# Single maxima behind each unit of scores and each weighing in the first softmax, in place of twos and threes behind a pair of key blocks

## The reference, cut to what matters

```
h = _layernorm(x) * (1 + ca) + sa
Q, K, V = proj(h)                       # 16 heads of 8, rotary on Q and K
scores = einsum('bhqd,bhkd->bhqk', Q, K) / sqrt(8)
scores = where(causal, scores, -1e10)
att = softmax(scores)                   # x is 4 batches of 512 tokens of 128
x = x + ga * (att @ V @ Wo + bo)
h = _layernorm(x) * (1 + cb) + sb
x = x + gb * ffn(h)                     # 16 experts, top 2
```

## Time and profile before

| | us |
|---|---|
| median of 3 runs | 442.27 |
| lowest, highest | 441.61, 442.72 |
| profiled execution, its own time | 441.48 |
| span of the profiled execution, first to last instruction | 439.70 |
| PE busy in the span | 353.3 |
| DVE busy | 298.0 |
| ACT busy | 242.2 |

### The profile page before, as it was taken

How to read it: one execution, slowest core, us unless ns; L and a number is a source line. 1 busy time by engine, 2 the same in 40 slices (tenths; PEclk the granted TensorE clock), 3 DMA queues, 4 the chain that set the end, 5 groups by cost and what they waited for, 6 DMA issues and landing times.

```text
span 439.7 us, 7235 instructions
## 1 busy us (share of the span) xinstructions
PE 353.3 (80%) x2652; PEld 164.3 (37%) x2684; DVE 298.0 (68%) x596; ACT 242.2 (55%) x291; POOL 111.2 (25%) x151
## 2 busy tenths in 40 slices
PE   0555386888867978999879969998879798879995
PEld 0532142445534444443444434433545323123122
DVE  7479994575878797777576877786549456943342
ACT  1102023344224786887534868875457887858970
POOL 8334720000524020443250204433130023122000
PEclk9996666999989999999998999999999999989999
DMA  8102410000220182554001715551105155704550
GB/s 291 25 1 68 79 46 24 3 5 0 50 29 2 39 106 71 137 143 110 2 25 31 95 51 141 135 133 22 28 0 73 36 144 160 117 2 121 151 135 24
DMA packets 26847, 31.43 MB, mean 71 GB/s; under 512 B 6454, under 2 KB 17718, under 8 KB 26678
## 3 DMA queue, kind: packets, MB, share of 16 engines
q1 hardware_dynamic: 23740, 28.84, 28.3%
q0 software_dynamic: 3072, 2.13, 2.8%
HBM read 3.47 MB, written 1.05 MB: 10 GB/s over the span
## 4 chain that ended last, share of the span: by engine, by line
PE 53%; DVE 19%; ACT 10%; issue 7%; SPq 4%; DMA 4%; POOL 1%; ACTq 0%; DVEq 0%; POOLq 0%
PE acc L1125 17%; PE big L1125 17%; PE misc L1125 17%; ACT ring L657 7%; DVE mx L897 6%; DVE xn L838 3%; DMA q_dense<-nm 2%; PE misc L1144 2%; SPq L425 2%; SPq L446 1%; ACT qk_turned L665 1%; SPq L380 1%; DVE stats L813 1%; DMA q_dense<-qk 1%; ACT L690 1%
## 5 line engine op out<-in xcount | busy, mean ns | idle before, releaser
L657 ACT ACTIVATE ring<-big 128x1024 f32<-128x1024 f32 (+1 forms) x224 | 197.3, 932 | 124.5 <-PE big L1125 123.2
L897 DVE TENSOR_REDUCE mx<-misc 128x1 f32<-128x320 f32 (+7 forms) x154 | 86.9, 589 | 36.0 <-PE misc L1125 34.6
L1125 PE MATMUL acc<-ring,cb 128*32 128x512 f32 x512 | 68.8, 612 | 5.4 <-ACT ring L657 4.4
L1125 PE MATMUL big<-tstack,w1s 128*128 128x512 bf16 x177 | 52.4, 381 | 10.0 <-ACT ring L657 7.1
L1125 PE MATMUL big<-q_dense,k_block 128*128 128x448 bf16 (+7 forms) x249 | 53.4, 320 | 5.2 <-DMA q_dense<-nm 3.1
L1125 PE MATMUL misc<-k_dense,q_block 128*128 128x384 bf16 (+7 forms) x171 | 43.6, 318 | 6.4 <-DVE mx L897 5.9
L1020 DVE SCALAR_TENSOR_TENSOR gm<-acc,cb,gm 128x512 f32<-128x512 f32 x40 | 29.9, 747 | 27.3 <-DMA gm<-wT 14.5
L1125 PEld LDWEIGHTS big<-q_dense,k_block 128*128 128x128 bf16 x256 | 30.8, 148 | 31.1 <-ACT ring L657 14.3
L1125 PEld LDWEIGHTS misc<-k_dense,q_block 128*128 128x128 bf16 x174 | 21.3, 149 | 52.1 <-DVE mx L897 37.0
L1125 PE MATMUL acc<-ring,vals 128*32 128x64 f32 (+7 forms) x512 | 40.1, 421 | 0.4
L1125 PE MATMUL big<-earlier_query,identb 128*128 128x64 bf16 (+2 forms) x176 | 37.0, 210 | 2.5 <-DMA q_dense<-nm 1.8
(11 more groups left out here) (160 smaller groups left out, 486.2 us busy)
## 6 DMA issues: line engine op xcount, KB each, us to landing
gm<-wT SPq DMA_DIRECT2D x64, 256.0 KB
tstack<-tp SPq DMA_DIRECT2D x18, 128.0 KB, 5.1
k_block<-qk_turned POOLq DMA_DIRECT2D x48, 32.0 KB, 3.6
q_dense<-qk SPq DMA_DIRECT2D x24, 64.0 KB
ca<-in_pack_a SPq DMA_DIRECT2D x1, 1155.0 KB, 5.4
k_dense<-qk SPq DMA_DIRECT2D x18, 64.0 KB
xs<-in_x SPq DMA_DIRECT2D x4, 256.0 KB, 8.0
q_block<-qk_turned SPq DMA_DIRECT2D x24, 32.0 KB
```

The lines of the kernel that those rows point to most:

```text
L657: act.activation(dst, src, func, scale=scale).then_inc(s["ring_read"], 1)
L897: dve.tensor_reduce(mx[:, g, k:k + n, blk], src, AX.X, ALU.max).then_inc(s["misc_read"], 1)
L1125: return pe.matmul(dst, lhsT, rhs, start=start, stop=stop)
```

## The change

`WOVEN` is now a table from a slot to units, where a slot is a unit of scores or one weighing. Behind most slots stands one unit of maxima, behind the weighings of key blocks 0 and 1 of each group two. Six units of the first batch move from the softmax into `ALONE` (of 384, 384 and four of 320 columns), one more unit of the second batch moves from `LEFT` into the softmax. `softmax` calls `between` behind each unit of scores and each weighing. PE's wait for batch 1's `k_dense` and `q_block` moves from key block (0, 4) to between `early_scores` and the rest of the softmax.

```
-ALONE = UNITS0[0] + UNITS0[1][:3] + [("mT", 0)] + UNITS0[1][3:10]
-REST = UNITS0[1][10:] + [("mT", 1)]
-WOVEN = {("first", 0, 0): REST[0:3], ("first", 0, 1): REST[3:6], ("first", 0, 2): REST[6:9], ("first", 0, 3): REST[9:12],
...
-LEFT = MAXIMA[30:]
+ALONE = UNITS0[0] + UNITS0[1][:3] + [("mT", 0)] + UNITS0[1][3:16]
+REST = UNITS0[1][16:] + [("mT", 1)]
+SLOTS = [("scores", 0, 4), ("scores", 0, 5), ("weigh", 0, 0), ("weigh", 0, 1), ("scores", 0, 6), ("scores", 0, 7),
...
+TWICE = [("weigh", 0, 0), ("weigh", 0, 1), ("weigh", 1, 0), ("weigh", 1, 1)]
+FIRST_SLOTS = SLOTS[:5]
...
+for slot in SLOTS[5:]:
+    n = 2 if slot in TWICE else 1
+    WOVEN["second", slot] = MAXIMA[at:at + n]
+    at += n
+LEFT = MAXIMA[at:]
...
                                 scores(phase, g * NU + u)
+                                if ("scores", g, u) in between:
+                                    between["scores", g, u]()
                         if len(late) == 2:
-                            weigh(m, phase, *late.pop(0))
-                            weigh(m, phase, *late.pop(0))
+                            for was in late:
+                                weigh(m, phase, *was)
+                                if ("weigh", *was) in between:
+                                    between["weigh", *was]()
+                            late = []
...
-                    if (g, blk) == (0, 4):
-                        for stack in ("k_dense", "q_block0", "q_block1"):
-                            wait_stacked(pe, stack, 2)
...
+            for stack in ("k_dense", "q_block0", "q_block1"):
+                wait_stacked(pe, stack, 2)
+            softmax(0, softmax_at(0), {slot: woven(slot) for slot in SLOTS})
```

## The result

| | before | changed |
|---|---|---|
| median of 7 runs each, us | 442.27 | 438.89 |
| lowest to highest, us | 441.61 to 443.58 | 437.90 to 441.26 |
| profiled execution, us | 441.48 | 438.46 |
| span of the profiled execution, us | 439.7 | 436.6 |
| first scores to last weighing in its first softmax, us | 42.6 | 38.8 |

The ratio of the changed kernel to the one before is 0.993, with a 95% interval of 0.9904 to 0.9956. The forecast was 439.4, within 437.0 to 441.4.

A forecast was written before the change was run, and what follows sets the result against it. PE was taken to bound the softmax, losing time in waits. 1.1 + 4.5 - 0.3 - 0.7 - 1.7 = 2.9 us gained, from the median of 442.27 to 439.4 us, range 437.0 to 441.4.

The forecast's parts named there:

- Part 1: Gap ahead of the first scores: six units of maxima fit in, covered by the `nm` DMAs; cost nothing, up to 0.3 us.
- Part 2: Ahead of unit 4: it begins at about 77.9 instead of 79.02, after waiting for `q_block`; gain 1.1 us.
- Part 3: Softmax: single units instead of twos and threes remove PE's waits for banks; 5.5 us shrink to 1.0, gain 4.5 us.
- Part 4: Softmax: one more unit costs 0.3 us, eight more places where a weighing follows a full-width matmul cost 0.7 us.
- Part 5: Behind the new `q_block` wait: PE's clock at half for 3.4 us, losing half of that, 1.7 us.
- full clock: Rival, chance 0.20: early scores and the short `q_block` wait do not bring the clock down; gain 4.6 us, 437.7.
- long half clock: Rival, chance 0.14: half clock behind the new wait lasts 6.8 us instead of 3.4; gain 1.2 us, 441.1.
- late landing: Rival, chance 0.05: `q_block` DMAs ahead of unit 4 land at 80.4, turning the 1.1 us into -1.5; 442.0.
- what follows: Rival, chance 0.05: the second batch's scores, behind the softmax, do not move with the last weighing; gain under 0.5 us, 442.0.
- slower case: Rival, chance 0.06: clock stays at half for 15 us behind the new wait, losing 7.5 us instead of 1.7; 445.2.

The follow-up runs named there:

- e4: The changed kernel with SP writing batch 1's `q_block` ahead of the first batch's `nm` of group 0; 435.71 us, 0.9848 of the kernel before.
- e5: The changed kernel with seven more matmuls of 512 columns ahead of PE's wait for batch 1's stacks; 439.08 us, 0.9913 of the kernel before.
- r1: The changed kernel, unaltered, timed again in another session; 439.37 us, 0.9925 of the kernel before.

## Why the prediction was right

The prediction held in its mechanism: an earlier unit 4, bank waits that go, and a half clock behind a new wait. The sizes are less good than the time makes them look. Measured with the traces and the experiments:

| part | forecast, us | measured, us | from |
|---|---|---|---|
| 1, six units into the gap | 0 | 0 | first scores at 71.93, `nm` 0.1 earlier as well |
| 2, earlier start of unit 4 | +1.1 | +1.2 | 79.02 to 77.85 |
| 3 and 4, waits gone, a unit and split pairs added | +3.5 | +3.7 | 35.5 to 31.8 at full clock (e4, e5) |
| 5, half clock | -1.7 | -1.2 and -1.5 | 33.0 and 33.3 (changed, r1) against 31.8 (e5) |
| sum | +2.9 | +3.7 (first trace) | |

The last weighing ends 3.9 us earlier (110.76), where 2.9 was forecast (111.7), an error of a third. The time is off by only 0.5 us (438.89 against 439.4), because what follows the softmax gave back part of the lead, which the prediction had at nothing. So the closeness of the time is in part luck.

- **Part 1** was right in its result and wrong in one expectation. The first scores are not late, but the clock fell all the same, at about 67.2, and was at half up to 74.1; I had expected the filled gap to keep it full. It cost nothing up to the first scores, which still begin when `nm` has landed. The early scores were through at 75.85, 0.5 us later than I had them, and nothing came of it, since PE then waited for `q_block`.
- **Part 2**: the last `q_block` DMA landed at 77.61, 0.2 us before the value taken. From its issue at 75.36 that is 2.25 us, so the choice of the shortest landing (2.3) was right; the median of 5.0 us would have been off by 2.8. The support that I gave for it was a misreading: the `nm` DMA that lands at 71.78 is the sixth, issued at 70.03, and took 1.75 us; the one issued at 69.40 is the fifth. Taken as it stands, the neighbour would have given about 77.1.
- **Part 3**: of the three waits that I had found in the new order, two came. The transposition waits 0.5 us in place of 0.4; the chain has one wait for ACT at scores 4 of the second group, and none for the second batch's transposition.
- **Part 4**: a split pair costs 0.14 us, and seven pairs 1.0 us, where I had 0.7 for eight. Parts 3 and 4 are measured only together, +3.7 for +3.5. If part 4 cost 1.0 and the unit's 0.3, an estimate, part 3 gained about 5.0 in place of 4.5.
- **Part 5**: 3.4 us at half clock, as expected, in both traces. It cost 1.2 and 1.5 us and not half of the stretch, 1.7: in the first trace 0.35 us of it lay in the idle wait, and a matmul's step is less than doubled (0.31 for 0.20 us). That is the term that was mis-sized.
- **The rivals**: full clock and long half clock did not come; the late landing did not come; what follows did move, by 4.0 us at the landing of `nm`. The slower case did not come.

The time gained less than the softmax: 3.8 us from the first scores to the last weighing, but 3.0 to 3.1 us in the span and 3.4 in the medians. DVE's copies of `yT`, one in each batch, show where it goes (the first three of before, then of the changed kernel):

```profile
132.71 0.69 DVE L936 COPY yT<-misc 128x512 f32<-128x512 f32 x1 [2.41 <-PE misc L1144]
221.90 0.68 DVE L936 COPY yT<-misc 128x512 f32<-128x512 f32 x1
312.97 0.68 DVE L936 COPY yT<-misc 128x512 f32<-128x512 f32 x1
```

```profile
129.15 0.69 DVE L952 COPY yT<-misc 128x512 f32<-128x512 f32 x1 [2.93 <-PE misc L1160]
218.36 0.68 DVE L952 COPY yT<-misc 128x512 f32<-128x512 f32 x1
307.79 0.68 DVE L952 COPY yT<-misc 128x512 f32<-128x512 f32 x1
```

The lead is 3.6, 3.5 and 5.2 us, and 3.1 at the end of the span. Ahead of the first `yT` the changed kernel has a longer stretch of half clock around the second batch's first scores, 6.8 us (121.9 to 128.7), where the kernel before has the 3.4 us from 128.3 of part 5; the second trace of the changed kernel has 6.8 us there too. The prediction left that place as it was. Between the second and the third, the execution of before had a stretch of half clock at 230.7 that the changed one has not; behind the third the changed one has two, from 319.8 and from 340.3, that the other has not. These later stretches lie in code that the change does not touch. They are what a single execution adds or takes, about 2 us either way, and why the parts were measured within the softmax. The changed kernel:

```profile
122.00:128.70 6.70, 4.31 (x18) 2.09 (x20) 3.08 (x6) 3.07 (x4) 1.22 (x3) 0.50 0.03 6
320.00:323.00 3.00, 2.78 (x23) 1.39 (x17) 0.14 (x1) 1.02 (x3) 0.00 (x0) 0.50 0.00 0
340.00:343.00 3.00, 2.49 (x7) 0.42 (x7) 0.28 (x1) 2.79 (x4) 0.00 (x0) 0.55 0.00 0
```

## What to carry to other kernels

When a wait is moved to an earlier place in a queue, work out when its DMAs land and put the wait next to the first instruction that reads the data, or issue the DMAs while their queue is idle: here that was worth about as much again as the whole change (e4 is 6.7 us under the kernel before, the changed kernel 3.1). With two buffers between PE and DVE, single pieces between other work beat groups of two and three here, but groups of two behind an unsplit pair of weighings were as good, since a split pair has its own price (0.14 us). Where PE was idle because ACT paced it, three pieces cost nothing; look for those places before placing them where the engine is the bound.

## What the runs showed of the hardware that was not expected

- PE's granted clock fell to half in a gap of 0.7 us. In the changed kernel PE was idle from 66.6 to 67.37, and the clock is at 0.50 from 67.5 to 74.0, although PE was busy 6.46 of these 6.5 us. In the kernel before, with the same gap (66.75 to 67.48), it stayed full until 70.2. In the second trace of the changed kernel it stayed full until 68.5. What decides between them is not shown.
- In the idle wait of 2.0 us the clock was still 1.00 from 76.0 to 77.4; the fall came at 77.5, near its end, and in the second trace at 78.8, when PE had worked again for 0.9 us. With 1.5 us of the wait filled with matmuls the clock stayed full behind it, in the one trace taken.
